# Gated cross-attention layer, 16 batches on one core: every queue of the last step written in another order

## The reference, cut to what matters

```python
x = x + tanh(g_xattn) * attention(layernorm(x), ctx)     # x: 16 x 512 x 512, ctx: 16 x 120 x 384
x = x + tanh(g_ffn) * quantised_layer(layernorm(x))
# attention: q = x@Wq+bq (16 heads of 32), k, v from ctx; softmax(q k^T / sqrt(32)) v; then @Wo + bo
# quantised_layer: scale = max(amax|x|, eps)/127; round(x/scale) @ W8^T (integers) * scale * w_scale + bias
```

## Time and profile before

| what | us |
|---|---|
| median of 3 executions (lowest, highest) | 791.55 (790.91, 792.83) |
| profiled execution, whole | 791.26 |
| its span, first to last instruction | 789.4 |
| TensorE busy in it | 767.4 (97%) |
| ScalarE, VectorE, GpSimd busy | 606.8, 542.5, 519.3 |

### The profile page before, as it was taken

One profiled execution on the slowest core, in us unless ns is written; L12 is line 12 of the kernel. 1 busy time (PEld: TensorE's weight loads), 2 busy tenths in 40 slices (PEclk: granted clock), 3 DMA queues, 4 the chain that ended last, 5 costly groups with the idle time before them and its releaser, 6 DMA issues.

```text
span 789.4 us, 16270 instructions
## 1 busy us (share of the span) xinstructions
PE 767.4 (97%) x5883; PEld 529.7 (67%) x5938; DVE 542.5 (69%) x863; ACT 606.8 (77%) x846; POOL 519.3 (66%) x546
## 2 busy tenths in 40 slices
PE   9999999999999999999999999999999999999996
PEld 6665667667666767767667766767667666766563
DVE  5977767666766767667765756766667765755568
ACT  5677789687787878778687786778788687787785
POOL 4445485775857569494775857569495775855588
PEclk9999999999999999999999999999999999999999
DMA  8678977987787887869778787987868777756722
GB/s 282 241 217 215 306 201 214 299 229 248 221 242 199 287 240 200 272 193 285 229 231 233 219 260 195 271 238 222 269 195 262 214 209 223 208 159 177 204 62 107
DMA packets 115199, 177.24 MB, mean 225 GB/s; under 512 B 35888, under 2 KB 45488, under 8 KB 113072
## 3 DMA queue, kind: packets, MB, share of 16 engines
q1 hardware_dynamic: 88336, 128.14, 52.9%
q10 hardware_dynamic: 26784, 48.06, 22.9%
HBM read 120.03 MB, written 56.13 MB: 223 GB/s over the span
## 4 chain that ended last, share of the span: by engine, by line
PE 91%; DVE 3%; issue 3%; POOL 1%; ACT 1%; ACTq 0%; DVEq 0%; POOLq 0%
PE bank_b L440 29%; PE bank_a L440 19%; PE scores L495 9%; PE sum_ps L544 8%; PE scores L536 7%; PE pv_ps L548 7%; PE bank_a L592 4%; PE bank_b L592 2%; PE bank_a L567 2%; PE scores L440 1%; DVE row_max L1363 1%; PE sum_ps L510 1%; PE pv_ps L836 1%; PE scores L470 1%; PE scores L518 0%
## 5 line engine op out<-in xcount | busy, mean ns | idle before, releaser
L1363 DVE TENSOR_REDUCE row_max<-scores 128x16 f32<-128x1920 f32 x64 | 137.9, 2154 | 19.0 <-PE scores L495 18.7
L1752 POOL TENSOR_TENSOR o_lo<-on,o_hi 128x512 fp32r<-128x512 f32 x48 | 62.3, 1298 | 115.0 <-ACT o_hi L998 115.0
L978 ACT ACTIVATE probs<-scores 120x2048 f32<-120x2048 f32 x64 | 120.1, 1876 | 21.9 <-PE scores L536 19.9
L1392 DVE SCALAR_TENSOR_TENSOR q_parts<-bank_b,bq_c,q_parts 128x512 fp32r<-128x512 f32 x44 | 33.0, 750 | 131.4 <-ACT q_parts L931 131.3
L495 PEld LDWEIGHTS scores<-k_sb,q_sb 32*128 32x128 f32 x1952 | 60.0, 186 | 51.6 <-issue 44.9
L1760 POOL TENSOR_TENSOR x<-x,gbias_r 128x512 f32<-128x512 f32 x64 | 82.9, 1297 | 16.6 <-ACT cen L1004 15.6
L1710 POOL TENSOR_TENSOR xt<-xt,rstd_b 128x512 f32<-128x512 f32 x56 | 85.4, 1561 | 2.4 <-issue 2.4
L1746 POOL TENSOR_TENSOR x<-x,gbo_r 128x512 f32<-128x512 f32 x64 | 81.9, 1291 | 3.8 <-DMA x<-in_x 3.7
L1765 POOL TENSOR_TENSOR x<-x,u_sb 128x512 f32<-128x512 f32 x56 | 72.8, 1300 | 4.8 <-DVE u_sb L1468 4.7
L440 PE MATMUL bank_b<-xt_hi,wq_hi 128*128 128x512 f32 x184 | 73.5, 400 | 0.0
L440 PE MATMUL bank_b<-xt_hi,wq_lo 128*128 128x512 f32 x184 | 72.6, 395 | 0.0
(11 more groups left out here) (246 smaller groups left out, 1951.1 us busy)
## 6 DMA issues: line engine op xcount, KB each, us to landing
q_stack<-q_rows ACTq DMA_DIRECT2D x180, 256.0 KB, 4.5
q_rows<-q_parts SPq DMA_DIRECT2D x60, 512.0 KB, 5.5
xt<-in_x_t SPq DMA_DIRECT2D x16, 1024.0 KB, 8.4
x<-in_x SPq DMA_DIRECT2D x64, 256.0 KB, 4.4
out_x<-x SPq DMA_DIRECT2D x61, 256.0 KB, 2.8
x_in<-in_x SPq DMA_DIRECT2D x60, 256.0 KB, 5.1
k_stack<-k_rows SPq DMA_DIRECT2D x90, 120.0 KB, 4.6
k_rows<-k_parts SPq DMA_DIRECT2D x30, 240.0 KB, 3.7
```

What stands on the lines that cost most here:

```text
L978: act.activation(probs[0:KEYS], scores[0:KEYS], ACT.Exp, scale=SCALE).then_inc(p_ready, 1)
L1363: dve.tensor_reduce(row_max[:].rearrange("p (t r) j -> p r t j", r=ROWG)[:, :, :, j], scores[:, :, 0:QT * KEYS].rearrange("p r (t k) -> p ...
L1752: pool.tensor_tensor(o_lo[i % 2][j], on[:], o_hi[i % 2][j].bitcast(F32), ALU.subtract).then_inc(o_split, 1)
```

## The change

Only the order changes: no instruction is added or removed. At the end of step 14 TensorE does the whole of `project_o(13,3)` ahead of `turn_max(15)`, where three of its twelve matmuls stood behind it; on VectorE `normalise_o(14,3)` moves from behind `dequantise(13,0)` to ahead of `maxima(15,3)`; on ScalarE `high_o(14,3)` moves from behind `copy_max(15)` to ahead of `high_max(15)`. In step 15 TensorE begins with `project_o(14,0)`, and the queues of TensorE, ScalarE and VectorE stand in a new order up to `normalise_o(15,3)`. Those of GpSimd and SyncE are as before.

```diff
@@ tensor: step, i = 14 @@
-                if is_batch(m) and i < LAST - 1:
+                if is_batch(m):
                     project_o(m, 3, bank_b)
-                if i == LAST - 1:
-                    for c in range(DT - 1):
-                        add_heads(m, 3, c, bank_b)
                 pe.wait_ge(log_done, nth(i, DT, 3))
                 turn_max(b, sum_ps)
-                if i == LAST - 1:
-                    add_heads(m, 3, DT - 1, bank_b).then_inc(proj_done, 1)
@@ tensor: last_step @@
-                pe.wait_ge(max_done, nth(i, DT, 3))
-                scores_by_key(i, 0)
                 pe.wait_ge(x1_ready, nth(e, QT, 3))
                 pe.wait_ge(o_split, nth(m, DT, 3))
                 project_o(m, 0, bank_b)
+                pe.wait_ge(max_done, nth(i, DT, 3))
+                scores_by_key(i, 0)
+                pe.wait_ge(u_ready, nth(e, QT, 1))
+                project_o(m, 1, bank_a)
                 pe.wait_ge(v_ready, nth(i, 1))
                 attend(i, 0)
                 scores_by_key(i, 1)
-                pe.wait_ge(u_ready, nth(e, QT, 1))
-                project_o(m, 1, bank_a)
+                pe.wait_ge(x1_ready, nth(m, QT, 1))
+                turn_z(e, 1, bank_a)
+                project_o(m, 2, bank_b)
                 attend(i, 1)
-                pe.wait_ge(x1_ready, nth(m, QT, 0))
-                turn_z(e, 1, bank_b)
                 scores_by_key(i, 2)
-                pe.wait_ge(x1_ready, nth(m, QT, 1))
-                project_o(m, 2, bank_a)
-                quantised_layer(e, 2, bank_b)
+                quantised_layer(e, 2, bank_a)
+                pe.wait_ge(x1_ready, nth(m, QT, 2))
+                quantised_layer(e, 3, bank_b)
                 attend(i, 2)
                 scores_by_key(i, 3)
                 pe.wait_ge(u_ready, nth(e, QT, 2))
-                quantised_layer(e, 3, bank_b)
-                pe.wait_ge(x1_ready, nth(m, QT, 2))
                 project_o(m, 3, bank_a)
                 attend(i, 3)
@@ scalar: step, i = 14 @@
+                if i == LAST - 1:
+                    high_o(i, 3)
                 if is_batch(b):
                     high_max(b)
...
-                high_o(i, 3)
+                if i < LAST - 1:
+                    high_o(i, 3)
@@ scalar: last_step @@
+                centre(e, 3)
+                spread_max(i)
                 exponentials(i, 0)
                 stack_q(i, 2)
-                spread_max(i)
-                centre(e, 3)
+                quant_round(e, 2)
+                quant_round(e, 3)
+                integers(e, 2)
+                integers(e, 3)
                 log_sums(i, 0)
                 invert_sums(i, 0)
                 exponentials(i, 1)
                 stack_q(i, 3)
-                quant_round(e, 2)
-                quant_round(e, 3)
+                copy_zt(e, 1, bank_a)
                 high_o(i, 0)
-                integers(e, 2)
-                integers(e, 3)
                 centre(m, 0)
                 log_sums(i, 1)
                 invert_sums(i, 1)
+                centre(m, 1)
                 exponentials(i, 2)
-                copy_zt(e, 1, bank_b)
-                centre(m, 1)
@@ vector: step, i = 14 @@
+                if i == LAST - 1:
+                    normalise_o(i, 3)
+                if is_batch(b):
                     maxima(b, 3)
...
-                normalise_o(i, 3)
+                if i < LAST - 1:
+                    normalise_o(i, 3)
@@ vector: last_step @@
+                residual(m, 0, bank_b)
                 quant_max(e, 2)
                 quant_max(e, 3)
                 quant_factors(e, 1)
-                normalise_o(i, 0)
-                residual(m, 0, bank_b)
                 x1_statistics(m, 0)
                 residual(m, 1, bank_a)
                 x1_statistics(m, 1)
+                normalise_o(i, 0)
+                residual(m, 2, bank_b)
+                x1_statistics(m, 2)
+                quant_max(m, 0)
                 normalise_o(i, 1)
-                quant_max(m, 0)
-                dequantise(e, 2, bank_b)
                 quant_max(m, 1)
                 quant_factors(m, 0)
-                residual(m, 2, bank_a)
-                x1_statistics(m, 2)
+                dequantise(e, 2, bank_a)
+                dequantise(e, 3, bank_b)
                 normalise_o(i, 2)
-                dequantise(e, 3, bank_b)
```

## The result

| kernel | median us (lowest, highest) | profiled execution, its span |
|---|---|---|
| before, 13 executions | 791.41 (790.40, 798.37) | 791.26, 789.4 |
| after, 13 executions | 794.01 (792.45, 795.99) | 794.93, 793.1 |

The ratio is 1.0027, interval [1.0015, 1.0039] (it isn't the ratio of the medians, 1.0033): 2.6 us longer by the medians, where 1.3 was forecast. The time lies inside the range and well above the likeliest value, so half of the difference has to be accounted for. Beside the order, `turn_z(13,1)`, `project_o(14,2)` and `quantised_layer(13,2)` now use the other one of `bank_a` and `bank_b`.

The account below looks back on a forecast made before the run. TensorE, busy 97% of the span, bounds the kernel: its queue plus its holes. The terms +2.5 - 2.7 + 1.5 = +1.3 us, on a median of 791.55, gave 792.8 us, range 790.2 to 794.3.

Parts of the forecast that it names:

- Term 1: End of step 14: ScalarE waits for `proj_done`, GpSimd holds `low_max`, so `quantised_layer(13,1)` starts 2.5 us later.
- The rival without the hold: End of step 14: `low_max` starts first and is not held by GpSimd; +0.2, 791.7 us; chance 0.2.
- The rival that ScalarE's wait costs nothing: End of step 14: the turn does not wait for `low_max`; -1.2, 790.4 us; chance 0.1.
- Term 2: From `quantised_layer(13,1)` to `attend(15,3)`: the old order's TensorE holes go, -2.7 us.
- Term 3: New hole at `attend(15,2)`, which waits for `normalise_o(15,1)`, now behind `quant_max(14,0)` on VectorE: +1.5 us.
- the forecast's lower bound of 0.7: Hole at `attend(15,2)` if only the exponentials hold it; as a rival +0.5, 792.0 us, chance 0.06.
- The slower rival: Step 15: a transfer start on ScalarE is slow and delays the chain to the end; +3.3, 794.8 us; chance 0.12.

Follow-up runs that it names:

- lo_behind_max: After, with GpSimd's `low_o(14,3)` made to wait until `low_max(15)` is done; 791.85 us, +0.74 against before.
- fill_hole: After, with 15 small unused matmuls on TensorE between `project_o(13,3)` and `turn_max(15)`; 792.05 us, +0.94 against before.
- only_step14: After with before's `last_step`, so that only the end of step 14 is changed; 793.14 us, +2.03 against before.
- dve_swap: After, with `normalise_o(15,1)` put back ahead of `quant_max(14,0)` on VectorE; 793.28 us, +1.74 against before.
- own_buffer: After, with batch 14's fourth group in two free slices of `xt_hi`, so `high_o(14,3)` needn't wait for `project_o(13,3)`; 790.11 us, -1.43 against before.
- own_swap: own_buffer plus the VectorE swap of dve_swap; 789.46 us, -2.08 against before.
- lo_swap: After with both edits, the extra wait of lo_behind_max and the swap of dve_swap; 791.01 us, -0.53 against before.
- only_last: Before with only the last step's queues (TensorE, ScalarE, VectorE) taken from after; 794.06 us, +2.95 against before.

## Why the prediction was right, and what it lacked

- **Term 1, +2.5:** measured +2.44. `low_max` took 1.24 (forecast about 1.3), `high_o` came at 733.56 - 0.71 = 732.85 (forecast 732.9). The rival without the hold (791.7) is refuted in after and was made to happen in lo_behind_max; its saving of 1.1 was 1.0. That GpSimd would be first rested on a lead of 0.1, worked out from differences as small as that; it was 0.11 in after and 0.10 in fill_hole, only_step14 and dve_swap.
- **The rival that ScalarE's wait costs nothing** (790.4) is refuted: it waited 3.72. own_buffer, which takes the wait away, gave -1.43, where that rival's sum was -1.2.
- **Term 2, -2.7:** neither wait for `low_o(14,3)` nor longer scores are left (1.09 at 741.62). The two account for 1.8 of the 2.7 (733.87 to 736.70, less 1.03). For the other 0.9 the prediction gave no reason: 0.7 of it stood at the quantised layer at 752.31 of before, which waited for `copy_zt`, and it is gone too, since the layer at 754.61 of after waits for nothing. It is confirmed in size by own_swap: with the first hole gone and 0.6 left of the second, -2.7 + 0.6 = -2.1, measured -2.08.
- **Term 3, +1.5:** measured 1.4, with the releaser that was named; the layer of 0.88 named above is outside it. dve_swap shows both what `quant_max` costs there (0.8) and what the exponentials alone would cost (0.6, the forecast's lower bound of 0.7).
- **The slower rival,** by starts of transfers on ScalarE, did not happen. The three starts behind the exponentials, in ScalarE's queue of after, take less than in the earlier trace rows, and no instruction of ScalarE in after waits for "issue" between 742 and 766 us:

```profile
742.81 1.28 ACTq L870 DMA_DIRECT2D q_stack<-q_rows  x3
```

- **The step that was missing:** the sum took a hole to cost its own length. The prediction put a block's cost behind the hole at the price of the full clock (2.87 for `project_o(14,0)`), as if every hole were like the one of 1.36 in step 15 of before, which left the clock alone; for one of 2.4 no bound was set. The trace of before had a sign of it at its very end, where the clock is at 0.50 from 2.8 us behind the last matmul on. The lowered clock cost 1.7 in the profiled execution. fill_hole shows that it is the clock, and lo_behind_max, lo_swap, own_buffer and own_swap that it goes with the hole. After's executions at 0.998 or more have a median of 792.97, near the forecast of 792.8; the median of all is above because eight of 13 are slower, most or all of them by this fall.
- **What was luck:** the range up to 794.3 was drawn without this term. That 794.01 still lies in it, 0.3 from its end, owes to a width that stood for other mechanisms.

How much of the 2.6 is the clock is known less well than the trace suggests: 1.7 by fill_hole's median, and 794.01 - 792.97 = 1.0 by the grouping of after's executions.

## What to carry to other kernels

Where a new order leaves TensorE idle for longer than anything in the middle of the trace did, let the range include a lowered clock: the blocks beside that hole priced at the lower level, here 1.7 us on a hole of 2.2. Before an order is given up, look at what its new wait hangs on: here a buffer shared by successive batches, and one instruction standing in VectorE's queue ahead of the one that TensorE needed, hid a gain of 2 us. (For the buffer this is shown with the new order alone.) And when two orders are compared, read who starts first where VectorE and GpSimd both come free by one ScalarE instruction: 0.1 us of lead was worth 1.0 us.

## What was not expected of the hardware

- Where the clock fell differs from trace to trace. In after and only_last it fell 1.0 and 1.3 us behind the hole, in the midst of work: in only_last TensorE came back at 736.41, ran five matmuls at the usual pace (a start every 0.23 to 0.31), and the slow ones begin at 737.66. In only_step14 and dve_swap it fell inside the hole, 0.3 and 0.25 ahead of its end, so that the turn already runs at 0.50 (1.09 us and not 0.63). Holes of 1.36 (before), 1.21 (lo_behind_max) and 1.22 (lo_swap) had no fall beside them; holes of 2.23 (after, only_step14, dve_swap) and 2.48 (only_last) had one, of 3.4 us or, in only_step14, of 6.8. These are one trace each, and nothing between 1.36 and 2.23 was run. By the mean clock it does not come every time: in at most eight of after's 13 executions.
- At the clock of 0.50 a matmul of 512 columns costs the queue 0.43 us (739.32 to 739.75 in only_last's timeline) and not 0.23. What TensorE lost was 1.7 us in after, about half of the 3.4 us that it worked at that level. In only_step14 it worked 6.5 us at that level, so half of it, about 3.3 us, is my estimate of its loss there.
- GpSimd's `low_o` began 0.11 ahead of `low_max` in after and held it for as long as it ran itself: the Trainium skill's rule ("SBUF — State Buffer", section "Who interferes with whom") that the first to start wins holds at that lead too, with an operand eight times narrower than GpSimd's.
